# Spare products with the identity on TensorE, beside normalisations, VectorE's steps and stage gaps

## The reference: what is computed

```python
x = x + _L0_xattn_ref(_layernorm(x, axis=-1), ctx_512, ...)
x = x + _L0_attn_ref(_layernorm(x, axis=-1), ...)
x = x + _L0_ffn_ref(_layernorm(x, axis=-1), ...)
...
x = x + _L3_ffn_ref(_layernorm(x, axis=-1), ...)
```

## Time and profile before

| | |
|---|---|
| median of 3 runs | 4842.14 us (4839.58 to 4857.5) |
| the profiled execution | 4844.16 us, its span 4842.4 us |
| mean granted TensorE clock | 0.916 |
| busy: TensorE, weight loads | 86%, 65% of the span |
| busy: VectorE, ScalarE, GpSimd | 53%, 37%, 16% |

### The profile page before, as it was taken

One profiled execution on the slowest core, in us unless ns is written; L12 is line 12 of the kernel. 1 busy time (PEld: TensorE's weight loads), 2 busy tenths in 40 slices (PEclk: granted clock), 3 DMA queues, 4 the chain that ended last, 5 costly groups with the idle time before them and its releaser, 6 DMA issues. The chain is left out here.

```text
span 4842.4 us, 106615 instructions
## 1 busy us (share of the span) xinstructions
PE 4176.4 (86%) x43882; PEld 3139.1 (65%) x43882; DVE 2561.9 (53%) x5119; ACT 1780.9 (37%) x3741; POOL 791.6 (16%) x476
## 2 busy tenths in 40 slices
PE   6869999999874979999876679776899899997988
PEld 4559888889554956666632379542699666665465
DVE  4268777777255045555439732346433566664443
ACT  2135555555221424444424312120444344443121
POOL 1022222221001200000019621015122000000300
PEclk8989999999885989999988889897799999999995
DMA  1010000000002831111012178558111100001000
GB/s 32 18 33 24 17 17 17 17 17 1 31 15 80 321 126 43 43 43 43 17 43 78 43 276 316 207 154 114 53 50 36 29 30 23 23 23 38 1 12 10
DMA packets 135776, 304.55 MB, mean 63 GB/s; under 512 B 51491, under 2 KB 86132, under 8 KB 117524
## 3 DMA queue, kind: packets, MB, share of 16 engines
q1 hardware_dynamic: 130900, 285.84, 18.8%
q0 software_dynamic: 4416, 12.06, 0.8%
HBM read 272.28 MB, written 23.47 MB: 61 GB/s over the span
## 5 line engine op out<-in xcount | busy, mean ns | idle before, releaser
L2777 DVE TENSOR_REDUCE block_max<-PS 128x1 f32<-128x512 f32 (+1 forms) x896 | 505.7, 627 | 300.1 <-PE PS L2637 299.5
L2726 ACT ACTIVATE probs_turned<-PS 128x512 f32<-128x512 f32 (+1 forms) x896 | 434.6, 571 | 559.8 <-PE PS L2658 559.7
L874 PE MATMUL PS<-context_turned,queries 128*128 128x422 f32 (+2 forms) x1536 | 342.6, 366 | 21.8 <-issue 18.3
L906 PE MATMUL PS<-probs_turned,context_part 128*128 128x256 f32 (+1 forms) x2496 | 331.9, 287 | 2.2 <-DVE weighted L985 2.2
L935 ACT CAST probs_turned<-PS 128x512 fp32r<-128x512 f32 (+1 forms) x512 | 232.1, 510 | 255.8 <-PE PS L886 255.8
L951 DVE TENSOR_TENSOR probs_turned<-PS,probs_turned 128x512 fp32r<-128x512 f32 (+1 forms) x512 | 276.6, 582 | 75.2 <-ACT probs_turned L935 73.3
L906 PEld LDWEIGHTS PS<-probs_turned,context_part 128*128 128x128 f32 (+1 forms) x2496 | 308.3, 189 | 2.4 <-DVE probs_turned L951 2.4
L874 PEld LDWEIGHTS PS<-context_turned,queries 128*128 128x128 f32 x1536 | 267.1, 194 | 51.1 <-issue 20.7
L2678 PEld LDWEIGHTS PS<-probs_turned,values 128*17 128x17 f32 x13312 | 191.2, 97 | 148.4 <-issue 121.6
L2637 PE MATMUL PS<-keys_turned,queries 32*128 32x512 f32 (+1 forms) x2048 | 241.5, 548 | 40.5 <-ACT probs_turned L2726 35.5
L943 ACT ACTIVATE probs<-PS,minus_max 128x844 f32<-128x844 f32 (+1 forms) x256 | 238.5, 932 | 94.5 <-DVE minus_max L996 92.8
(11 more groups left out here) (529 smaller groups left out, 7407.9 us busy)
## 6 DMA issues: line engine op xcount, KB each, us to landing
context_rows<-in_ctx SPq DMA_DIRECT2D x40, 768.0 KB
context_turned<-ctx_turned SPq DMA_DIRECT2D x32, 800.5 KB
routed_up<-in_L_ffn_W SPq DMA_DIRECT2D x23, 1024.0 KB
routed_down<-in_L_ffn_W SPq DMA_DIRECT2D x23, 1024.0 KB, 5.2
routed_up<-in_L_ffn_wg_w SPq DMA_DIRECT2D x23, 1024.0 KB
routed_second<-in_L_ffn_w_w SPq DMA_DIRECT2D x23, 1024.0 KB
routed_down<-in_L_ffn_w_w SPq DMA_DIRECT2D x23, 1024.0 KB, 5.0
v_all<-v_turned SPq DMA_DIRECT2D x128, 128.0 KB, 19.7
```

The lines of the kernel that those rows point to most:

```text
L874: last = nc.tensor.matmul(PS[:, j, 0:cols], qs[a][:, v, p * P:(p + 1) * P], yT[b][:, v, at:at + cols], start=(m == 0), stop=(m == 2))
L906: last = nc.tensor.matmul(O_ps, yp[a][0:kk, u, k, :], probsT[b][0:kk, par, k, :], start=(k == 0 and m == 0), stop=(k == KT - 1 and m == 2))
L2726: nc.scalar.activation(probs[0:kk, t % ring, i, 0:many].rearrange("p k c s -> p (k c s)"), PS[0:kk, bank_of("turned", t, i), 0:many * 2 * ...
L2777: nc.vector.tensor_reduce(part[:, b % 2, chunks[0]:chunks[-1] + 1, i, u // 2], bank, AX_X, ALU.max).then_inc(max_done.sem, 1)
```

## The change

A helper `spare_products` issues n float32 products of the identity with the identity's first 64 columns repeated to 256, into a bank that nobody reads. They are put on TensorE:

- in every `normalize`: 1 at the start of the block, 1 after each of the first three `norm_stats` of either half, 2 after the variance is ready; with a gain 6 more, one for every second of VectorE's scaled tiles; without gain and with transposes 2 before the first half's transposes and 1 before the second's;
- in every `vector_steps`: `busy` products (1, 2 or 3) at each step, each step's waiting for the step before; 4 in `scalar_step`; 4 in `top_two`;
- in `self_attention`: 2 after the first scores, 2 after the first maximum, 2 (6 with a mask) after the second scores;
- in `routed_experts`: 10 after the prefix products, 8 after the table, 14 at the end, once all slots' results have been taken.

Nothing is removed.

```diff
+def spare_products(core, bank, n, cols=256):
+    for _ in range(n):
+        core.nc.tensor.matmul(core.PS[:, bank, 0:cols], core.ident[:], core.ident[:, 0:SEQ].unsqueeze(1).broadcast_to([P, cols // SEQ, SEQ]),
+                              start=True, stop=True)
...
@@ normalize
-            if turned is not None:
-                @block.tensor
-                def _(pe):
+            spare = BANKS - 1
+            @block.tensor
+            def _(pe):
+                spare_products(core, spare, 1)
+                for h, tiles in enumerate(tile_halves):
+                    for m in range(3):
+                        pe.wait_ge(stats_done.sem, stats_done.at(2 * h * len(tiles) + m + 1))
+                        spare_products(core, spare, 1)
+                pe.wait_ge(var_ready.sem, var_ready.at(len(tile_halves)))
+                spare_products(core, spare, 2)
+                if gain is not None:
+                    for t in range(0, 2 * TILES - 4, 2):
+                        pe.wait_ge(step.sem, step.at(t + 1))
+                        spare_products(core, spare, 1)
+                if turned is not None:
                     for f in range(fills):
                         half, c = f // chunks, f % chunks
+                        if c == 0 and gain is None:
+                            pe.wait_ge(step.sem, step.at(4 * half + 1))
+                            spare_products(core, spare, 2 - half)
                         if c == 0:
...
-def vector_steps(core, steps):
+def vector_steps(core, steps, busy=1):
...
+        @block.tensor
+        def _(pe):
+            for n in range(len(steps)):
+                if n:
+                    pe.wait_ge(step.sem, step.at(n))
+                spare_products(core, BANKS - 1, busy)
...
@@ self_attention
                 scores(0)
+                spare_products(core, t_bank + 1, 2)
+                pe.wait_ge(topped.sem, topped.at(1))
+                spare_products(core, t_bank + 1, 2)
                 for i in range(TILES):
                     if i + 1 < TILES:
                         scores(i + 1)
+                    if i == 0:
+                        spare_products(core, t_bank + 1, 2 if mask is None else 6)
...
@@ scalar_step
+        @block.tensor
+        def _(pe):
+            spare_products(core, BANKS - 1, 4)
...
@@ top_two
+        @block.tensor
+        def _(pe):
+            for n in range(0, 2 * TILES, 4):
+                if n:
+                    pe.wait_ge(step.sem, step.at(n))
+                spare_products(core, BANKS - 1, 1)
...
@@ routed_experts
                                  stop=True).then_inc(prefix.sem, 1)
+                spare_products(core, spare_bank, 10)
                 pe.wait_ge(parts_ready.sem, parts_ready.at(2))
...
                 last.then_inc(map_ready.sem, 1)
+                spare_products(core, spare_bank, 8)
...
                     last.then_inc(bias_ready.sem, 1)
+                    pe.wait_ge(y_moved.sem, y_moved.at(SLOTS))
+                    spare_products(core, spare_bank, 14)
```

More of the change, by code:

```diff
@@ L446, in add @@
 def add(core, dst, a, b):
-    vector_steps(core, [lambda: core.nc.vector.tensor_tensor(dst[:], a[:], b[:], ALU.add)])
+    vector_steps(core, [lambda: core.nc.vector.tensor_tensor(dst[:], a[:], b[:], ALU.add)], 3)
 def self_attention(core, qT, kT, V, O, heads, d, dv, scale, mask=None, minus_lam=None):
@@ L1359, in l0_xattn @@
                         vector_steps(core, [lambda: nc.vector.tensor_tensor(R[:], R[:], U[:], ALU.add),
-                                            lambda: nc.vector.tensor_tensor(X[:], X[:], R[:], ALU.add)])
+                                            lambda: nc.vector.tensor_tensor(X[:], X[:], R[:], ALU.add)], 3)
 def value_affine(core, wv, gain, shift, scaled, bias):
@@ L1430, in l0_attn @@
             lambda: v.tensor_reduce(var[:], U4, AX_X, ALU.add),
-            lambda: v.tensor_scalar(var[:], var[:], 1.0 / dv, EPS, ALU.mult, ALU.add)])
+            lambda: v.tensor_scalar(var[:], var[:], 1.0 / dv, EPS, ALU.mult, ALU.add)], 3)
         scalar_step(core, lambda: nc.scalar.activation(var[:], var[:], ACT.Sqrt))
@@ L1436, in l0_attn @@
             lambda: v.tensor_tensor(O4, O4, along(w["L0_attn_ln_g"]), ALU.mult),
-            lambda: v.tensor_tensor(O4, O4, along(w["L0_attn_ln_b"]), ALU.add)])
+            lambda: v.tensor_tensor(O4, O4, along(w["L0_attn_ln_b"]), ALU.add)], 3)
         turn(core, O, DC, uT)
@@ L1834, in routed_experts @@
     up_names = ("up", "second") if mult else ("up",)
-    x_bank, y_bank, small_bank, bias_banks = 4, 5, 7, (2, 3, 4, 7)
+    x_bank, y_bank, spare_bank, small_bank, bias_banks = 4, 5, 6, 7, (2, 3, 4, 7)
     step, ones_made, counted, prefix = (core.semaphore("vector_step"), core.semaphore("ones_made"), core.semaphore("counted"),
@@ L3607, in cut @@
             return v.tensor_tensor(x, x, masks["width_turned"][:, c, :].unsqueeze(1).broadcast_to([P, BATCH, SEQ]), ALU.mult)
-        vector_steps(core, [(lambda c: lambda: cut(c))(c) for c in range(DC)])
+        vector_steps(core, [(lambda c: lambda: cut(c))(c) for c in range(DC)], 2)
         linear_turned(core, uT, w["q_w"], qT, w["q_b"])
@@ L3614, in l3_ffn @@
         rows_mask = masks["width_rows"][:].unsqueeze(1).broadcast_to([P, TILES, DIM])
-        vector_steps(core, [lambda: v.tensor_tensor(O[:], O[:], rows_mask, ALU.mult)])
+        vector_steps(core, [lambda: v.tensor_tensor(O[:], O[:], rows_mask, ALU.mult)], 3)
         turn(core, O, DC, uT)
```

## The result

The changed kernel took 4827.0 us in the median of eight runs (4819.4 to 4840.1), beside 4843.6 us in eight runs of the kernel before. The ratio is 0.9965, with a 95% interval of 0.9948 to 0.9982: 16.5 us faster, within half a per cent, where I had forecast 38 us. The profiled execution took 4825.9 us.

A forecast was written before the change was run, and what follows sets the result against it. TensorE was taken as busy 86% of the span, with scattered half-clock time, much of it idle or in untouched waits. Terms summed to -33, plus -5 for chance: 4806 from 4844.2, 4804 against the median; stated 4805, 8-in-10 range 4772 to 4830.

The forecast's parts named there:

- Short steps cost: Softmax, `scalar_step`, `top_two` in routed layers: products in 0.2 us steps cost +4 for both; l2_ffn's steps and softmax +5.
- the other two routers: Two biased or bare routers would run faster for part of their length: -2.5 us.
- The table: Routed experts, two layers: 32 records of 7.10 us gain at most 3.5 each at full clock; half counted, -3.5.
- Norms: Normalisations: transposes at full clock gain 1.2 us in seven stages, -8.4; first products behind norms -6.
- Output rows of l3_ffn: Dense products and transposes ahead bring full clock; eight tiles go from 3.15 to 1.55 us each: -12.8 us.
- my first rival: Clock holds, but l3_ffn's output rows are reached at half clock and first self-attention falls back: 4822 us, chance 0.22.
- Self-attention of l3_ffn: Half-clock products delay the first tile by up to 3.7 us; a few faster tiles give that back: 0.
- more comes back: l3_ffn's attention holds full clock (-9), l2_attn's rows too (-7 more): 4789 us, down to 4768; chance 0.15.
- First self-attention: Masked self-attention: period falls from 7.90 to 5.69 us for three slow periods, less delayed transposes: -6 us.
- Chance: Stages whose clock depends on how the fall lands, chiefly l2_attn's output rows (-12 at a chance of 0.4): -5 us.
- The rule that transposes don't count: In norms and l3_ffn's turn, transposes let the clock fall, losing those gains: 4833 us, chance 0.03.
- the slower rival: Products don't raise the clock and pace at half clock in norms and short steps: 4932 us, chance 0.04.

The follow-up runs named there:

- the kernel with trimmed norms: Changed kernel without short-step products, 17 before the table, covers before V's and l2_attn's rows, six beside l3_ffn's cut, three fewer per gainless norm: 4785.3 us, ratio 0.9890.

## Why the prediction was wrong

The direction was right and the size twice too large. By the steps of the forecast:

- **Short steps cost.** This is the step that failed. "About 12 products a layer, +1 at full clock and +3.5 when entered at half: +4 for both", and +5 in l2_ffn: 9 us. They cost 16.1 by places, in kernels whose times differ by 18 to 25 us. I had the price of a product right (nine in 7.12 us, between my 4.0 and 9). But I let the cost of the l0 and l1 routers be the products less a cover, and there is no cover: VectorE's steps take 0.2 us each, a block ends only with its last engine, and the next block's first instruction waits for it. I also took back 1.5 us in l2_ffn for a clock that its gate products then did not have. The 2.5 us for the other two routers did come for the most part (1.5 and 0.7; as first products behind a norm, those of l0_ffn stand with the norms in the table).
- **The table.** I counted half of 7 us although I had seen that the products may end 2 to 4 us early. They ended 4.33 and 4.39 us early, and the gain was 0 in both layers. Seven more products made it 3.3 and 2.2 us at the table, of which some 2 us in all were left once the first slots were done. That the wait for the gather behind the table grows when the table gets faster was missing from my sum.
- **Norms.** The mechanism was right (1.04 us for eight transposes), the size too large: 8.7 us in place of 14.4. The first products behind the norms gave 5.1 us in three stages (1.3, 1.7 and 2.1) and little elsewhere, where I had 6. That leaves some 3.6 for the norms themselves, where I had 8.4: six gave 0.74 to 1.0, two lost 1.1 each. I had let the second eight transposes start at VectorE's end and take 0.97; they start 0.19 later and take 1.04, and that they do so with three fewer products too shows that the spare products are not what holds them.
- **Output rows of l3_ffn.** Right in its size (-11.6 with turn and cut, against -12.8; the rows come 1.69 us apart and not 1.55), and three products alone bring it. What I had not seen is that the state is a near thing: my first rival, that the rows are reached or left at half clock, happened in three of twelve profiles. In the changed kernel neither of that rival's conditions came about, so that its 4822 lies near the measured 4827 is chance.
- **Self-attention of l3_ffn.** I had 0 and it gave 6.9. My rival "more comes back" had it at 9: a tile's period fell from 4.70 us to between 3.0 and 3.4. Four products behind the first scores and two behind the second were enough to raise the clock, and small tiles then kept it for 24 us. I had argued from their staying at half clock that they would not.
- **First self-attention.** Right in its mechanism and near in size (-7.8 with the stage behind, against -6). Its masks are 5.69 us apart from the second one on, as forecast.
- **Chance.** I added -5 for a clock that falls elsewhere; it came to +2.6 (among it l1_xattn's head attention +4.0, l2_attn's rows +0.4 and still at 0.50 in the rows above, context attention -3.7). A term that has no mechanism should have been 0. l2_attn's rows were to be had, but by a product in the wait before them, not by luck.
- **The rule that transposes don't count** as work for the clock (the Trainium skill, TensorE: Matmul & The Clock Gate, Part 4) was given 0.03. The kernel with transposes as fillers has 515 us at half clock against 499 with products and 813 with none. On this chip, in fp32, they count.
- **Pace at half clock** (the slower rival) would have needed 0.6 us a product. They took 0.45 at full clock and 0.86 at half (from start to start), in norms mostly the first.

## What to carry to other kernels

Filling an engine's wait to keep its clock pays only where the filler ends before the wait does and the next real work on that engine is on the path: price the filler against the shortest wait it stands in, not against the mean one, and put none into steps of 0.2 us. Put it last in the wait, up against the work that it is for: ten products that ended 4.3 us ahead of a table bought nothing there, seventeen that ended 3.0 and 1.3 us ahead bought 2.2 and 3.3, and three to ten that ended about a microsecond before dense rows bought 10 to 12 us each in most profiles, though not in all. Then look at the wait behind the work: if that one only grows, little is kept. Half-clock time that goes away is no measure of the gain (314 us of it gave 18 us), so find the few stages where TensorE is both slow and the bound, and treat those alone.

## What the runs showed of the hardware

- A fall of the clock can follow dense work at full clock. In the kernel with trimmed norms 4.25 us of products, in which the clock rose, and 1.94 us of transposes at full clock were followed by a wait of 1.05 us and rows with bias products of one partition, and the clock fell in the second tile of these, some 2 us in. The same rows in other kernels kept full clock for all of 13.5 us. I found no difference in what TensorE did in the microseconds ahead that would explain it; this stays open.
- Tiles with mostly small products (32 and 64 rows), busy 21.4 of 26.0 us, keep for a while a clock that they do not raise: in the changed kernel it is 1.00 from 4764 to 4788 us and falls in the last tile, and it is 0.50 over the whole stage where no spare product stands in it.
- One kernel's runs differ by up to 43 us on one chip (4810 to 4853 for the kernel before), more than most single edits here are worth. In one pair of profiles 10.9 us of such a difference arose in a stage that the edit had not touched.
